# Two-layer decoder kernel: third norm's statistics, GpSimd's scatter and the gate's projection placed elsewhere in the first phase

## The reference, cut to what matters

```python
x = x + L0_attn(layernorm(x))             # state-space mixer: conv, decay, gate
x = x + L0_xattn(layernorm(x), ctx, ctx)  # 16 heads, masked softmax over the context
x = x + L0_ffn(layernorm(x))              # shared expert + the best 2 of 16 routed ones

# in the mixer
x_ssm, z, B_in, C_in, dt_in = split(layernorm(x) @ in_proj_w.T)
x_ssm = silu(causal_conv(x_ssm)); dt = softplus(dt_in + dt_bias); a = exp(A * dt)
h = a * h + dt * B * x;  y = C . h + Dp * x           # 32 heads, per token
y = rmsnorm(y) * norm_w * silu(z);  out = y @ out_proj_w.T
# in the feed-forward part
probs = softmax(xn @ Wr); two largest -> routed rows; shared = (silu(xn@Sg) * (xn@Su)) @ Sd
```

## Time and profile before

| what | value |
|---|---|
| time, median of 3 runs | 4862.58 us (4860.41 to 4864.49) |
| the profiled execution: its time, its span | 4860.3 us, 4858.7 us |
| busy over the span | TensorE 88%, VectorE 67%, ScalarE 59%, GpSimd 55% |
| first phase, whole iterations (215.5 to 2434.1 us) | TensorE busy 1900.04 of 2218.60 us, mean granted clock 0.82 |
| second phase (2570 to 2900 us) | TensorE busy 288.27 of 330.00 us, clock 0.94 |
| third phase (2900 to 4858 us) | TensorE busy 1914.83 of 1958.00 us, clock 0.99 |

### The profile page before, as it was taken

How to read it: one execution, slowest core, us unless ns; L and a number is a source line. 1 busy time by engine, 2 the same in 40 slices (tenths; PEclk the granted TensorE clock), 3 DMA queues, 4 the chain that set the end, 5 groups by cost and what they waited for, 6 DMA issues and landing times.

```text
span 4858.7 us, 118978 instructions
## 1 busy us (share of the span) xinstructions
PE 4291.8 (88%) x33430; PEld 3114.9 (64%) x33431; DVE 3260.6 (67%) x8668; ACT 2883.9 (59%) x6966; POOL 2670.3 (55%) x4092
## 2 busy tenths in 40 slices
PE   3888888888888888888868979999999999999998
PEld 2666666666666666666646756666666666666665
DVE  2666666666666666666634547777777777777776
ACT  2566666666666666666633436666666666666664
POOL 3666566656665666555522235555555555555554
PEclk8888788878887888888879989999999999999999
DMA  5222222222222222222204410111111111111110
GB/s 154 70 92 77 74 74 88 81 73 75 83 85 74 75 78 88 77 75 73 83 27 146 143 58 28 31 31 31 31 31 31 31 31 31 31 31 31 30 31 19
DMA packets 215890, 304.15 MB, mean 63 GB/s; under 512 B 56608, under 2 KB 167456, under 8 KB 215840
## 3 DMA queue, kind: packets, MB, share of 16 engines
q1 hardware_dynamic: 188864, 240.33, 15.7%
q0 software_dynamic: 19200, 52.45, 3.3%
q10 hardware_dynamic: 7776, 10.75, 0.7%
HBM read 239.19 MB, written 64.23 MB: 62 GB/s over the span
## 4 chain that ended last, share of the span: by engine, by line
PE 68%; DVE 10%; issue 9%; POOL 5%; ACT 5%; DMA 1%; DVEq 1%; SPq 1%; POOLq 0%; ACTq 0%
PE Q L1395 20%; PE Q L1388 14%; PE Q L1400 11%; PE Q L1423 4%; PE Q L1432 3%; PE Q L1735 3%; PE Q L1768 3%; PE Q L1589 3%; DVE mx L767 2%; ACT arena L1225 2%; PE Q L1601 2%; PE Q L1417 1%; ACT arena L1145 1%; DVE arena L847 1%; PE Q L1487 1%
## 5 line engine op out<-in xcount | busy, mean ns | idle before, releaser
L1400 PE MATMUL Q<-ident,arena 128*128 128x128 f32 x4768 | 805.0, 295 | 382.8 <-ACT arena L1145 260.4
L1400 PEld LDWEIGHTS Q<-ident,arena 128*128 128x128 f32 x4768 | 561.0, 147 | 661.3 <-ACT arena L1145 299.8
L616 POOL TENSOR_TENSOR arena<-arena 128x1024 f32<-128x1024 f32 x256 | 482.6, 1896 | 90.1 <-DMA arena<-cum_rows 89.1
L1395 PE MATMUL Q<-Wkvl,arena 128*128 128x512 f32 x1024 | 499.6, 600 | 0.0
L680 POOL TENSOR_TENSOR l<-l,half_pow 128x8 f32<-128x8 f32 x192 | 318.5, 1659 | 237.5 <-DVE l L1025 235.7
L644 POOL DMA_INDIRECT routed_rows<-arena,meta x128 | 150.7, 1178 | 461.8 <-DVE meta L912 439.1
L705 POOL TENSOR_TENSOR arena<-arena,part_of 128x512 f32<-128x512 f32 x256 | 263.8, 1041 | 194.4 <-DVE part_of L1063 194.3
L767 DVE TENSOR_REDUCE mx<-Q 128x4 f32<-128x512 f32 x512 | 350.1, 684 | 9.0 <-PE Q L1417 4.3
L1417 PE MATMUL Q<-arena 32*128 32x128 f32 x4096 | 331.9, 309 | 0.0
L1423 PE MATMUL Q<-ident,arena 128*128 128x128 f32 x2048 | 313.3, 295 | 17.8 <-ACT arena L1162 16.0
L1417 PEld LDWEIGHTS Q<-arena 32*128 32x128 f32 x4096 | 315.0, 221 | 7.2
(11 more groups left out here) (308 smaller groups left out, 10418.9 us busy)
## 6 DMA issues: line engine op xcount, KB each, us to landing
arena<-cum_rows SPq DMA_DIRECT2D x256, 512.0 KB, 6.0
arena<-routed_rows SPq DMA_DIRECT2D x144, 128.0 KB, 2.1
expert_rows<-arena POOLq DMA_DIRECT2D x144, 128.0 KB, 2.0
arena<-in_x_dram SPq DMA_DIRECT2D x128, 128.0 KB, 2.1
arena<-in_ctx_dram SPq DMA_DIRECT2D x128, 128.0 KB, 2.1
x_rows<-arena SPq DMA_DIRECT2D x128, 128.0 KB, 1.7
arena<-x_rows SPq DMA_DIRECT2D x128, 128.0 KB, 2.3
out_dram<-arena SPq DMA_DIRECT2D x64, 128.0 KB, 1.7
```

Of the source, the lines that this page charges most:

```text
L616: tell(g.tensor_tensor(E8[j], E8[j], cums[:, 8 * j:8 * j + 8].unsqueeze(2).broadcast_to([P, 8, T]), ALU.subtract), "diff")
L1395: last = mm(out, lhs(c), rhs(c), start=c == 0, stop=c == n - 1)
L1400: last = nc.tensor.transpose(out[:, c * P:(c + 1) * P], src[:, c * P:(c + 1) * P], ident[:, :])
```

## The change

Three things move in the tables of the first phase; no arithmetic is added or taken away.

1. The statistics of the third norm on VectorE (bn_stats, bn_aggr) and its `centre` on GpSimd leave chain F, where they stood in the iteration after x2, and become the last part of chain X, in the iteration that makes x2: on VectorE as step Xln3 between Xho and Vcv3, on GpSimd as step Xln3 behind Nrms. ScalarE's and TensorE's part (Fln3, Fln3n) stay where they are.
2. GpSimd's order around the scatter is `Mln1 Nm3 Msp Fsc Yx1r` instead of `Mln1 Fsc Nm3 Msp Yx1r`.
3. TensorE runs Vz and Vzh together and YcT after them (before: Vz YcT Vzh); ScalarE takes Vtz before YcT (before: YcT Vtz).

The counters (`signals`, `links`) follow the steps.

```diff
 "POOL":
-    Nd0 Nd1 Nd2 Fln3 Nd3 Mln1 Fsc Nm3 Msp Yx1r Yln2 Nyg Nrms
+    Nd0 Nd1 Nd2 Nd3 Mln1 Nm3 Msp Fsc Yx1r Yln2 Nyg Nrms Xln3
 "DVE":
-    Fln3 Xm0 Xm1 Mln1 Yln2 Nm0 Nm1 Fr Xm2 ... Vcv2 Fxo Xho Vcv3 Ny0 Vxs2 Ny1 ...
+    Xm0 Xm1 Mln1 Yln2 Nm0 Nm1 Fr Xm2 ... Vcv2 Fxo Xho Xln3 Vcv3 Ny0 Vxs2 Ny1 ...
 "ACT":
-    Yq YcT Vtz NyT Yv
+    Yq Vtz YcT NyT Yv
 "PE":
-    NyT Vz YcT Vzh Yk Yv VCB Npr Nprh
+    NyT Vz Vzh YcT Yk Yv VCB Npr Nprh
...
 # GpSimd
+            def X(b):
+                yield "ln3"
+                centre("ln3", mvF, b, "X_POOL")
+
             def F(b):
-                yield "ln3"
-                centre("ln3", mvF, b, "F_POOL")
                 yield "sc"
...
 # VectorE, end of chain X
                 tell(v.tensor_tensor(x2, x1r, o0, ALU.add), "x2")
+                yield "ln3"
+                done(dve, "x2", b)
+                moments("ln3", x2, stF, mvF, "X_DVE", b)
...
             def F(b):
-                yield "ln3"
-                done(dve, "x2", b)
-                moments("ln3", x2, stF, mvF, "F_DVE", b)
                 yield "r"
```

More of the change, by code:

```diff
@@ L53 @@
         "POOL": """
-            Nd0 Nd1 Nd2 Fln3 Nd3 Mln1 Fsc Nm3 Msp Yx1r Yln2 Nyg Nrms
+            Nd0 Nd1 Nd2 Nd3 Mln1 Nm3 Msp Fsc Yx1r Yln2 Nyg Nrms Xln3
         """,
         "DVE": """
-            Fln3 Xm0 Xm1 Mln1 Yln2 Nm0 Nm1 Fr Xm2 Ftop Fslot Mdt Nm2 Msp Xm3 Fhg Vcv0 Vcv1 Vcv2 Fxo Xho Vcv3 Ny0 Vxs2 Ny1 Vxdt Vgz Yk Vcb Nx1
+            Xm0 Xm1 Mln1 Yln2 Nm0 Nm1 Fr Xm2 Ftop Fslot Mdt Nm2 Msp Xm3 Fhg Vcv0 Vcv1 Vcv2 Fxo Xho Xln3 Vcv3 Ny0 Vxs2 Ny1 Vxdt Vgz Yk Vcb Nx1
         """,
@@ L287, in two_layers @@
         signals("Y", "POOL", "x1r ln2_rstd")
-        signals("X", "DVE", "S0max:4 x2")
+        signals("X", "DVE", "S0max:4 x2 ln3_var")
         signals("X", "PE", "S0:4 PT0ps:4 PV0:2")
         signals("X", "ACT", "mrow P0:4 PT0s:4 OT0")
-        signals("F", "DVE", "ln3_var rmax sel slot hh xo")
+        signals("F", "DVE", "rmax sel slot hh xo")
         signals("F", "PE", "ln3_Tps rout rank gu hTps down")
         signals("F", "ACT", "ln3_xn ln3_T rexp gth hT")
-        signals("F", "POOL", "ln3_rstd")
+        signals("X", "POOL", "ln3_rstd")
         for s in range(DEEP):
@@ L319, in two_layers @@
         signals("T", "POOL", "lno_rstd ln7_rstd")
-        links = {"M_DVE": 3, "V_DVE": 3, "Y_DVE": 1, "X_DVE": 4, "F_DVE": 15, "A_DVE": 5, "C_DVE": 1, "K_DVE": 2, "T_DVE": 7, "M_POOL": 13, "N_POOL": 1, "Y_POOL": 3,
-                 "F_POOL": 3, "A_POOL": 1, "C_POOL": 2, "K_POOL": 4, "T_POOL": 2}
+        links = {"M_DVE": 3, "V_DVE": 3, "Y_DVE": 1, "X_DVE": 5, "F_DVE": 14, "A_DVE": 5, "C_DVE": 1, "K_DVE": 2, "T_DVE": 7, "M_POOL": 13, "N_POOL": 1, "Y_POOL": 3,
+                 "X_POOL": 3, "A_POOL": 1, "C_POOL": 2, "K_POOL": 4, "T_POOL": 2}
         steps = {}
@@ L645, in F @@
                          "scattered", 16)
-            program(pool, "POOL", 1, (("M", M, 0), ("N", N, 1), ("Y", Y, 2), ("F", F, 4)))
+            program(pool, "POOL", 1, (("M", M, 0), ("N", N, 1), ("Y", Y, 2), ("X", X, 3), ("F", F, 4)))
             met(pool, "POOL", 1)
```

## The result

The changed kernel took 4954.5 us (median of 4 runs, 4951.1 to 4957.7) against 4861.6 us: a ratio of 1.019, 95% interval 1.0177 to 1.0202. It is 93 us slower where 4862 was forecast. The profiled execution took 4957.7 us with a span of 4956.1.

What follows compares the result with a forecast made beforehand. The prediction took a chain of waits across engines, with TensorE partly at half clock, as the bound. Terms -0.15 + 0.11 + 0 - 0.45 + 0.64 = +0.15 us a period would be absorbed by the clock's rise: 4862 us, range 4836 to 4892.

Steps and rivals of the forecast that it cites:

- the scatter's move: GpSimd's scatter issued behind the series, ahead of x1r: 0 us a period, ends -0.1 and +0.4.
- The held pace: First phase: the clock's rise shifts to meet period sums between some -0.7 and +0.7 us, keeping 37.6 us.
- the gate's +0.64: TensorE's Yk, waiting for ScalarE's copy behind the tanh, starts 0.64 us later a period; ends 0 and +0.98.
- The sign that the prediction took for a pace: Clock rises 37.54 us apart, with x1 spacings of 37.08 and 37.77, read as the program being pulled back.
- The terms of the statistics: Third norm's statistics: -0.15 us a period from leaving the iteration's top, +0.11 for the second norm's scaling.
- The hold: GpSimd's L583 no longer held by VectorE's product L824: -0.45 us a period, ends -0.6 and 0.
- the gains stay and the pace isn't held: Rival, first phase: the copy hides behind something, -0.49 us a period, 4834 us; chance 0.14.
- The clock no longer falls: Rival: shorter TensorE idle time before the third norm's transposes avoids half clock, -3.4 us a period, 4660 us; chance 0.06.
- The context's copy becomes the wait: Rival: Yk behind the tanh costs 0.64 us, the earliest rise can't compensate, +0.60 a period, 4898 us; chance 0.18.

Runs made afterwards that it cites:

- stats_only: Kernel before with only the third norm's statistics moved, scatter and gate orders as before: 4809.3 us, 0.9893.
- scatter_only_again: Unedited repeat, on another chip, of the kernel before with only the scatter moved behind the series: 4872.4 us, 1.002.
- stats_scatter: Changed kernel with the gate's orders as before, so statistics and scatter moved: 4874.8 us, 1.0029; its repeat on another chip 4880.9 us, 1.0036.
- after_again: The changed kernel again, unedited, on another chip: 4947.5 us, 1.0169 of the kernel before.
- stats_fill_top: Kernel with only the statistics moved, plus 14 filler matmuls on TensorE ahead of the third norm's transposes: 4813.5 us, 0.9899 of the kernel before.
- scatter_mid: Kernel with the statistics moved and the gate as before, scatter issued between L620 and the series: 4816.2 us, 0.9903 of the kernel before.
- scatter_only: Kernel before with one edit, GpSimd issues the scatter behind the series: 4916.7 us, 1.0116.
- extra_indirect: Kernel before with its scatter in place and a second, indirect scatter into a spare table added behind the series: 5067.8 us.

## Why the prediction was wrong

**The step that failed** is the scatter's move, "the scatter is issued by 1028.6 to 1029.0, and x1r needs x2 at 1028.81: I take 0, with ends -0.1 and +0.4". Measured it is 0.2 us a period alone, 1.1 to 1.2 on top of the statistics, and 1.5 to 1.6 on top of both other edits. The times in it were nearly right: the issue ends 25.4 us after x1 (25.6 in the period shown), forecast 24.9 to 25.3, and x2 of the earlier trace rows is ready at 25.13. What was wrong is that I compared them in one period of the kernel before, with a late rise of the clock. The issue ends at a nearly fixed distance from x1, because GpSimd's last long wait is for ScalarE's exponential (L1201), 13.1 us after x1 (1013.51), and the series behind it always takes as long; x2 moves with the clock and with the other edits: it ends 25.1 us after x1 in the earlier trace rows and 23.4 to 25.1 in stats_only. So the scatter isn't a term of a sum but a floor under x1r, the earliest time at which it can start. Added to the kernel before it puts x1r at 25.66 instead of 25.2 on average, and the periods with one fall at 37.75 instead of 37.53: 59 x 0.22 is 13 us, measured 9 (the median of scatter_only_again). Added to stats_only it puts x1r at 25.43 instead of 24.5, and the periods with one fall at 37.36 instead of 36.69: 40 us. Measured are 65 and 72 (stats_scatter and its repeat, less stats_only); the second falls, 1.1 to 1.3 us each in 17 and 11 of 54 periods, are the rest in the traces. On top of the gate as well it is 86 to 93 us: x1r comes at 25.4 instead of 24.4, and 49 of 54 periods have a second fall instead of 21. That the floor brings the falls, by keeping an early TensorE waiting, is my reading and not shown: the same wait comes with and without one.

**The held pace was half true.** "Sums between some -0.7 and +0.7 would be met too." On the slow side the gate's +0.64, measured +0.71 in a period with the same fall and rise as before (the period of after_again from 1117.01, 37.92, against 37.08 of the earlier trace rows, of which 0.13 is the second norm's), was met: 3 us in all, with 10.4 us at half clock instead of 13.8. On the fast side nothing was held: the statistics gave 52 us, and took the same shorter stretch at half clock (three of four periods have 10.2 us). So the slack could be used once, by the gate or by the statistics; after the statistics the gate's projection, free before, cost 52 us, and the scatter 65 to 93. The sign that the prediction took for a pace is none: in stats_only too 41 of 55 rises of the clock come 37.5 us after the one before, at a mean period of 36.76.

**The terms of the statistics were near, and more came of them.** In a period of stats_only with the fall and rise of before (from 947.93; 37.07 us against 37.08) strips 2 and 3 came 0.38 us earlier (0.29 forecast), the cross attention 0.10 (0.15), and the second norm's scaling not at all (+0.11 forecast, on top of the -0.15). Beside a period of before without the hold nothing is gained there. The hold was real: in the kernel before L583 is held in 33 of 54 periods, which take 37.71 us, and 13 free ones with the same single fall take 37.07; in stats_only none is held. That is 0.6 x 33/54 = 0.4 us a period (0.45 forecast, with three of four). The other 0.5 comes in the three of four periods, mostly 36.4 to 36.65 us, in which the clock now rises 13.5 to 15.8 us after x1. That would have been the rival "the gains stay and the pace isn't held", 4834 us at 0.14, and for the statistics alone it was the right one. An early x2 gives little of itself: with x2 ready at 23.54 the period is 36.50, with 24.57 it is 36.65 (from 985.01 and 1058.10), and `a` is ready at 24.1 in both. I take GpSimd's series to be the second floor there; no run tests it.

**The rivals.** "The clock no longer falls" did not come: the first fall stayed in every kernel. Its price of 3.4 us a period stays open; 5 us less at half clock between 3 and 8 us after x1 made good the 1.25 us that stats_fill_top's filler cost, and no more. "The context's copy becomes the wait" had the right place and price (0.64 forecast, 0.67 to 0.71 measured), but not its condition: the other edits had to use up the early rise first. Its 4898 us is met by no kernel. None of the rivals had two edits that each cost little against the kernel before and much on top of the third, and that is what happened: -52, +52, +86 to +93. The stated range, 4836 to 4892 us, also leaves out the very numbers of the two rivals that it was said to take in, 4834 and 4898.

**Best version.** stats_only, at 0.9893 [0.9877, 0.991] of the kernel before, beats both kernels (scatter_mid, 0.9903 [0.9883, 0.9923], can't be told from it); the gate's new order and the scatter's new place are better left out.

**Still open.** Why the signals were late on some chips and what that cost scatter_only; what decides whether a period has the second fall.

## What to carry to other kernels

Price a moved step against the earliest time at which its successor can be ready, not against that of one recorded period: an issue at a fixed distance from the iteration's start is a floor, harmless until another edit makes the rest faster. Where a period can take up a delay, as the gate's here, edits are not additive; the first spends the slack, so build them one by one and in pairs before a sum is believed. Compare neighbouring periods of one trace that differ in one thing, here a fall of the clock: that gave the price that a filler could not. And repeat a strange observation on another chip before it becomes a cause.

## What the runs showed of the hardware

On at least two chips TensorE's signals came late beside an indirect DMA's issue: 1.52 us (median) for the sum in the changed kernel's first trace, 0.75 in scatter_only, 1.88 for Nv3 in extra_indirect, where transposes beside the issue were late too, by 0.46; not with plain DMAs. On three others it was 0.01 us for the sum, in the changed kernel and scatter_only too, with the scatter and the sum at the same distances from x1. In the profile such a wait has "remote" as its releaser. The Trainium skill (SBUF — State Buffer, Who interferes with whom) says that "PE and ACT never wait on anyone"; the second trace agrees (0.01 us), the first does not if it is the matmul that waited, and whether it was that or the signal's way no row shows.

What half clock costs depends on where it falls: 3.4 us of it behind the second norm made a period 1.0 us longer (38.38 against 37.39), while 5 us less of it between 3 and 8 us after x1, with a filler of 1.25 us, left the time at 4813.5 us against 4809.3.
